# Moving GpSimd's gathers of expert rows by a slot or two in a three-phase transformer kernel

## What is computed

```python
x = x + LN(attn0(LN(x)))                 # 16 heads of 8, causal
h = LN(x)
h = h + attn1(LN(h));  h = h + token_moe(LN(h))   # each token: top 2 of 8 experts
h = h + attn2(LN(h));  h = h + seq_moe(LN(h))     # each sequence: top 2 of 8 experts
out = x + LN(h)
```

## Time and profile before

| | |
|---|---|
| median of three runs | 1174.61 us |
| the profiled execution, its time | 1179.62 us |
| its span, first to last instruction | 1177.6 us |
| TensorE busy | 87% |
| VectorE busy | 78% |
| ScalarE busy | 66% |
| GpSimd busy | 60% |
| mean granted TensorE clock | 0.961 of full speed |
| phase three with its pipeline full | from about 778.7 to 1009.1 us of the span |

### The profile page before, as it was taken

The page is one execution under the profiler, slowest core; times in us unless marked ns, Lnnn a source line. Parts: engine busy times, 40 slices in busy tenths (PEclk is TensorE's granted clock), DMA queues, the critical chain, the costliest instruction groups (busy, mean ns, idle before and its releaser), DMA issues. The chain is left out here.

```text
span 1177.6 us, 34922 instructions
## 1 busy us (share of the span) xinstructions
PE 1025.1 (87%) x10453; PEld 796.5 (68%) x10453; DVE 920.7 (78%) x2712; ACT 780.4 (66%) x1908; POOL 701.0 (60%) x1034
## 2 busy tenths in 40 slices
PE   1799999999999999998199998288898998989996
PEld 0567676676676766665199998166666665768986
DVE  4679999999989999997647665378898888856675
ACT  1577777777787777775078886167677776755564
POOL 3356666666667888886623332677787786533332
PEclk9999999999999999999589999699999999989999
DMA  5343122221212222221122222244222222100000
GB/s 147 101 113 83 51 56 54 53 56 52 54 51 61 65 66 65 64 68 34 54 62 69 66 70 74 65 126 124 70 63 65 59 65 53 48 2 15 19 19 22
DMA packets 120406, 73.71 MB, mean 63 GB/s; under 512 B 10688, under 2 KB 115264, under 8 KB 120256
## 3 DMA queue, kind: packets, MB, share of 16 engines
q1 hardware_dynamic: 101600, 53.12, 16.5%
q10 hardware_dynamic: 14560, 10.35, 3.2%
q0 software_dynamic: 4096, 8.40, 2.5%
HBM read 21.68 MB, written 11.60 MB: 28 GB/s over the span
## 5 line engine op out<-in xcount | busy, mean ns | idle before, releaser
L616 DVE TENSOR_REDUCE wide<-bank 128x2 f32<-128x512 f32 (+1 forms) x576 | 388.7, 678 | 55.4 <-PE bank L307 40.4
L503 ACT ACTIVATE prob<-bank 128x512 f32<-128x512 f32 x576 | 337.4, 592 | 89.2 <-PE bank L329 58.9
L902 POOL TENSOR_SCALAR_AFFINE_SELECT prob<-prob 128x512 f32<-128x512 f32 x384 | 249.9, 657 | 105.3 <-ACT prob L503 103.4
L348 PE MATMUL bank<-prob,vaug 128*32 128x256 f32 (+1 forms) x3072 | 166.9, 335 | 5.7 <-ACT oT L509 3.2
L1237 POOL COPY w_job<-w_s 128x512 f32 x104 | 67.9, 654 | 154.6 <-PE bank L1206 153.6
L315 PE MATMUL bank<-stack 126*128 126x256 bf16 x768 | 149.8, 276 | 0.0
L334 PE MATMUL bank<-stack 128*128 128x256 bf16 x768 | 148.4, 274 | 1.4 <-ACT prob L503 1.4
L1228 ACT ACTIVATE prob<-bank,b_job 128x128 f32<-128x128 f32 (+1 forms) x416 | 132.5, 400 | 23.7 <-PE bank L1206 12.3
L1217 PE MATMUL bank<-w_job,prob 128*128 128x128 f32 x1088 | 139.7, 276 | 1.9 <-issue 1.8
L348 PEld LDWEIGHTS bank<-prob,vaug 128*32 128x32 f32 x3072 | 81.7, 110 | 80.3 <-issue 48.4
L1217 PEld LDWEIGHTS bank<-w_job,prob 128*128 128x128 f32 x1088 | 132.1, 192 | 4.9 <-issue 3.6
(11 more groups left out here) (183 smaller groups left out, 2073.1 us busy)
## 6 DMA issues: line engine op xcount, KB each, us to landing
stack<-parts SPq DMA_DIRECT2D x576, 64.0 KB
w_s<-e_w ACTq DMA_DIRECT2D x32, 256.0 KB, 3.0
oT<-x_routed SPq DMA_DIRECT2D x72, 64.0 KB, 1.8
y_routed<-oT SPq DMA_DIRECT2D x36, 128.0 KB, 1.9
stack<-mT SPq DMA_DIRECT2D x192, 4.0 KB
out<-x_all SPq DMA_DIRECT2D x16, 128.0 KB, 1.8
b_all<-e_b ACTq DMA_DIRECT2D x2, 512.0 KB, 8.3
x_routed<-hk,x_at POOLq DMA_INDIRECT x64
```

Source lines behind the costliest of these rows:

```text
L348: m = nc.tensor.matmul(o, w, (prob0, prob1)[kb][:, g % 2, h], start=kb == 0, stop=kb == 1, skip_group_check=True)
L503: nc.scalar.activation(o, s, ACT.Exp, scale=SCALE).then_inc(exp_done, 1)
L616: nc.vector.tensor_reduce(o, s, AX.X, ALU.max, negate=True).then_inc(max_done, 1)
L902: nc.gpsimd.affine_select(out=t, in_=t, compare_op=ALU.is_ge, fill=0.0, base=0, pattern=[[0, HG], [1, P]], channel_multiplier=-1).then_inc ...
```

## The change

Only the block in `pool_slot` that issues the gathers is changed. In a step, the first slot now issues piece 2 of the item three steps ahead, the second slot issues none, the third slot issues piece 3 of it, and the fourth slot issues pieces 0 and 1 of the item four steps ahead. In the very first step of the pipeline pieces 0, 1 and 2 of the first item all go out in the first slot.

```diff
@@ pool_slot
             if k == 3 and nxt and nxt.phase == 2:
                 pool_bias(nxt)
-            nxt3 = item(step, 3) if step_phase(step) == 2 else None
-            if nxt3:
-                pool_fetch(nxt3, k)
+            if step_phase(step) == 2:
+                d, pieces = {0: (3, (2,)), 1: (3, ()), 2: (3, (3,)), 3: (4, (0, 1))}[k]
+                if step[0] == step[3] - 3 and d == 3:
+                    pieces = range(pieces[-1] + 1) if k == 0 else pieces
+                for n in pieces:
+                    if item(step, d):
+                        pool_fetch(item(step, d), n)
             sending = first if k == 3 else item(step, -5)
```

## The result

The changed kernel takes 1159.64 us, the median of four runs (1158.54 to 1160.75), against 1173.79 us for the kernel before in four runs (1172.34 to 1177.23): a ratio of 0.9875 with a 95% interval of 0.985 to 0.9901. It is 14.15 us faster. The forecast was 1162, in a range of 1152 to 1173.

A forecast was written before the change was run, and what follows sets the result against it. VectorE was taken as the path, held by waits for GpSimd's gathers and `post_r`. Twelve steps going from 17.81 to 16.5 us gave 15.7, less 0.4 at the start: 1164.3 or 1159.3, so 1162 us, range 1152 to 1173.

The forecast's parts named there:

- The last piece: Piece 3 moves from fourth to third slot, about 3.2 us earlier: VectorE's 16.0 us gather wait goes, 14 to 15 in twelve steps.
- The second slot's gather: With it gone from ahead of `post_r`, that begins some 1.1 us earlier; 6 of VectorE's 7.7 us wait go.
- The fourth slot: Two gathers there end at 831.1 instead of 829.02; GpSimd's idle time and the departed gather absorb the delay: cost nothing.
- One sign of being wrong: TensorE's line 348 waiting for line 902, listed among what would show the prediction wrong.
- the margin: TensorE's product with the values, second slot: its slack behind the first slot's selects shrinks from 1.7 to 1.1 us.
- What bounds the new step: Phase three's step: TensorE 16.1 us, GpSimd 15.9, VectorE 15.8; 16.1 plus 0.4 gives 16.5.
- VectorE's term: VectorE's part of a new phase-three step: 15.48 us busy in the mean plus 0.3 of gaps, 15.8.
- The 0.4 that I added: Allowance on the new phase-three step of 16.1 us, because three engines within 0.3 us do not run at the largest figure.
- The basis: Time the gain is taken from: the profiled execution, 1179.6 us, gives 1164.3; the median, 5.0 us lower, gives 1159.3.
- The start: Three gathers instead of two ahead of the first `pre_r`: 0.35 us lost, perhaps as much given back; booked +0.4.
- The slower one: Rival, 7%: two fourth-slot gathers make TensorE's product with the values wait; 16 us in every other step, 1190 us.
- The waits move: Rival, 10%, no change: VectorE waits for TensorE or `post_r` instead; only two long steps shorten, by 5.3 us: 1169.3 to 1174.3.

The follow-up runs named there:

- the last piece alone: Kernel before with only piece 3 moved, from the fourth slot to the third beside piece 2; pieces 0 and 1 stay: 1166.06 us, ratio 0.9909.
- the simple shift: Kernel before with every piece issued one slot earlier, so that the second slot keeps a gather (piece 2): 1160.65 us, ratio 0.9872.
- without any copy the simple shift: Every piece one slot earlier than in the kernel before, and GpSimd's copy of the row numbers and its wait left out: 1158.99 us, ratio 0.9854.
- four-piece order: Kernel before with all four gathers and the copy in the fourth slot, for the item four steps ahead: 1177.85 us, ratio 1.0018.
- two orders with an empty second slot: Kernel before with the second slot's gather moved to the first slot (1182.55 us) or the third (1185.93 us), piece 3 still in the fourth.
- order with pieces 1 and 2 in the third slot: Kernel before with the second slot's gather moved to the third slot, piece 3 still in the fourth: 1185.93 us, ratio 1.0077.
- kernel before without the copy: Kernel before without GpSimd's copy of the row numbers and the wait for it; gathers read the full table: 1179.09 us, ratio 1.0023.
- Without the copy: Changed kernel without GpSimd's copy of the row numbers and the wait for it: 1156.40 us, ratio 0.9841; again 1155.42 us, ratio 0.9827.

## Why the prediction was right

**The last piece.** Right, and the larger part: a wait of 16.0 us to none, and done alone worth 10.5 us in the twelve steps of its profile. The prediction let 14 to 15 go; done alone it gives some 4 of them back, as the wait for `post_r` is 7.1 us longer and 3.2 us of gather wait are left.

**The second slot's gather.** The sum of this term was about right and its reason only half. I counted 6 us for it; the changed kernel is 6.5 us better in the twelve steps than the last piece alone. But the simple shift, with a gather still in the second slot, gets 5.5 of them. What both orders share is less between GpSimd's wait for ScalarE in the first slot and `post_r`: less the copy in the one order, less copy and a gather in the other. That this is what counts is argued and not shown; without any copy the simple shift has more wait for `post_r` (12.6 us), not less, in shorter steps. And the term was no gain by itself: with the last piece late the kernel lost 0.6% and 0.8%.

**The fourth slot.** Right. The two gathers there cost nothing, the selects of the first slot run together at 843.58, and TensorE doesn't wait for them. One sign of being wrong, line 348 waiting for line 902, did appear, at 0.3 us a step, but in the third slot and for a select that stands ahead of `post_r`; the prediction had not looked there. The four-piece order shows that the margin is real and that TensorE's product with the values is who pays.

**What bounds the new step.** The forecast was 16.5 us, the mean of the twelve is 196.69 / 12 = 16.39, eight of them about 16.23. The prediction had three engines within 0.3 us and put TensorE first, at 16.1. It is GpSimd, which I had at 15.9: with 14.08 busy, its bracketed waits in the stretch above and the rows between sum to 2.0 us, and I had counted 1.76; the 0.24 for ScalarE's cast in the second slot was left out. VectorE's term was the furthest off. I had 15.48 busy, the mean of the kernel before with its long steps in it, although the mean of the two ordinary steps that I named is 15.06, and kept 0.64 us a step either way. It measured 14.28, 1.2 lower. The 0.4 that I added for the engines getting in each other's way was too much for GpSimd and stood in for what was missing there. So 16.5 came this close partly by luck: the engine named first was not the bound, and the allowance covered it.

**The basis.** The profiled execution is 5.0 us above the median, and I wondered whether its long steps were rarer in other runs. In the one other run that was profiled they are not. The second profile of the kernel before, 7.6 us shorter, has its first gather at 731.0 us instead of 735.3, so 4.3 of these lie ahead of phase three and 2.2 in the twelve steps. Against that profile's 211.45 the gain in the twelve steps is 14.8, close to the 14.15 of the medians.

**The start.** I booked 0.4 us of loss. From the first gather to the first `onT` copy it is 60.11 us before and 59.26 after, but 59.29 in the second profile of the kernel before, and 59.34 and 61.60 in two more of the changed kernel. It varies by over 2 us in one and the same kernel, so a cost of 0.4 can't be seen.

**The rivals.** The slower one has its mechanism in the four-piece order. It costs 15.3 us in the twelve steps there, against the changed kernel; the prediction's 16 us were to come on top of the kernel before. "The waits move" came true in part: VectorE waits for TensorE, but in a shorter step. The gathers took 943 to 1134 ns in the changed kernel, with two in a row in each step. The fivefold one of the Trainium skill's page "SBUF — State Buffer", section "A bandwidth-pool intuition that's wrong", is not to be seen in them either.

## What to carry to other kernels

Where an engine of low mean share feeds the path, follow its order of work through one whole step: place its movable work where it would wait for another engine anyway, and count from there what stands ahead of each result that is waited for. Waits that follow each other on one engine are not to be added up; removing the second first may bring nothing, as in the two orders with an empty second slot. When a wait has gone, close the new step by adding the next engine's busy time and all the short waits that it makes itself: GpSimd, at 60% busy over the span, had only such short waits left in a step of phase three, and 1 us less on it in each step was worth 3 to 4.6 us of the kernel. Moving one engine's work also moves which instructions of two engines meet, and that can cost more than the move saves: look at the instructions of the path that got longer.

## What the runs showed of the hardware

**A long step is three things in a row.** First, the gather lands late. DMA queues of the kernel before, from 846.5 to 849.2 us, while the last piece of the long step is under way:

```profile
q1 hardware_dynamic: 180, 0.09, 13.3%
q0 software_dynamic: 32, 0.07, 9.3%
q8 instruction: 1, 0.02, 2.3%
```

An instruction packet runs beside the 32 packets of the gather. From 829 to 830.8 us, in an ordinary step, there is none:

```profile
q1 hardware_dynamic: 232, 0.11, 22.0%
q0 software_dynamic: 32, 0.07, 13.5%
```

The rows came 2.79 us after GpSimd was done in the first case, 1.74 in the second. In both profiles of the kernel before, every landing of over 2.0 us had an instruction packet in its time (there are packets beside landings of 1.6 to 1.8 as well). In the order with pieces 1 and 2 in the third slot, one landing of 2.15 (792.34) had none. So that is a coincidence seen again and again, not a cause tested by itself.

Second, VectorE, come late, meets GpSimd's `rest`. Kernel before, VectorE and GpSimd in order of time (L625 starts 0.34 us before the end of the gather that stands ahead of `rest`):

```profile
850.46 1.56 DVE L625 TENSOR_TENSOR wide<-wide 128x8 bf16<-128x8 f32 x1
```

```profile
849.83 0.97 POOL L946 DMA_INDIRECT y_got<-y_routed,y_at  x1 [0.82 <-ACT prob L503]
850.82 1.17 POOL L911 TENSOR_TENSOR rest<-qkf,parts 128x512 f32<-128x512 f32 x1
```

An instruction on 8 elements a partition, which takes 0.17 us where nothing is in its way, lasts 1.56 and ends 0.03 us after `rest` does. Third, TensorE, which needs its result, stops for 2.98 us, and behind it the granted clock is 0.50 from 853 to 856, the lower of its two levels (1.2 GHz), so the mean of the step is 0.91. The two matmuls of L315 at 853.03 take 0.64 us and take 0.38 at the higher level (2.4 GHz). But the stop is what costs. The second profile of the kernel before has the same two long steps, with stops of 2.97 and 2.96 us and the clock low behind the first alone:

```profile
841.67:861.34 19.67, 16.53 (x179) 12.11 (x177) 16.49 (x38) 12.75 (x30) 14.04 (x21) 0.91 0.22 58
964.36:984.01 19.65, 15.41 (x179) 11.19 (x177) 16.29 (x38) 12.81 (x31) 14.05 (x21) 1.00 0.23 60
```

**The second link alone is enough.** In the kernel before without the copy `rest` comes 1 us earlier. In the step below the last piece lands 1.64 us after GpSimd is done, no later than in ordinary steps, and VectorE meets `rest` all the same. VectorE, GpSimd and TensorE:

```profile
883.33 1.41 DVE L625 TENSOR_TENSOR wide<-wide 128x8 bf16<-128x8 f32 x1
```

```profile
883.53 1.17 POOL L911 TENSOR_TENSOR rest<-qkf,parts 128x512 f32<-128x512 f32 x1
```

```profile
884.84 0.27 PE L359 MATMUL bank<-identb,wide 128*128 128x128 bf16 x2 [2.28 <-issue]
```

```profile
880.66:899.56 18.90, 15.39 (x180) 11.18 (x177) 16.77 (x38) 12.83 (x30) 14.09 (x20) 1.00 0.24 62
```

Four steps of this run have such a stop, of 2.04 to 2.28 us (in two of them the last piece landed in 1.6 to 1.7 us, in two in 2.2 to 2.3). In three the clock stayed at 1.00 and the step took 18.89 to 18.90; in the fourth it was 0.91 and the step took 19.00. So nearly all of what such a step costs is the stop, and not the clock. In the step of 21.11 the late gather (2.93 us) and the meeting are both there, and it is L797 that is long, 2.48 us at 973.02 instead of 0.61. The meetings use up what the ordinary steps gain. But the twelve steps are not longer in sum than in the kernel before, so the 0.2% that this version lost are not seen in them. From the first gather to the first `onT` copy this profile has 63.94 us, against 60.11 and 59.29, and its first L797 there takes 2.79 us (776.08). Whether that stretch is as long in the other runs is not known. The Trainium skill, page "SBUF — State Buffer", section "Who interferes with whom", has GpSimd and VectorE share a pair of ports under an exclusive lock; the ends of L625 here, each within 0.05 us of the end of GpSimd's instruction, agree with it. Meetings still occur in the changed kernel. L625 takes 1.2 us beside two selects in a row in two of the twelve steps of its first profile and in eight of another, and some 0.5 beside one select in most of the rest; the ordinary steps of that other one are 16.2 us all the same, and VectorE has time to spare there.

**Left open.** The changed kernel's first two steps are 16.78 and 16.79 us and its eighth is 16.75, with GpSimd no busier. In the first two the DMA engines are busy for 0.45 of the time with expert weights instead of 0.25. What makes these steps longer was not tried. In the eighth, GpSimd's second gather starts at 908.18, 0.98 us after the first has ended instead of 0.30, and so it does in two more profiles of the changed kernel; nothing in the profile shows what held it. Without the copy the eighth step is 15.88 to 15.89, like its neighbours.
